# Splitting three of four second products of a macaron block's experts into reduced-precision parts, scans included

## The chip, the cores and the metric

The kernel runs on one core of one Trainium2 chip. The metric is device time in microseconds (us) of one launch; lower is better. TensorE is called PE below, VectorE DVE, ScalarE ACT, GpSimd POOL and SyncE (which here only issues DMAs) SP, as in the profile.

## The reference

Hidden states of 2 x 1024 tokens by 128 channels pass through half a mixture of experts, an attention layer with a recurrent state, and the same half mixture of experts again (same weights):

```python
x = x + 0.5 * ffn(layernorm(x))
x = x + attn(layernorm(x))
x = x + 0.5 * ffn(layernorm(x))

# ffn: 8 experts, all computed, two kept by a gate; F = 512
top_w, top_idx = top_k(softmax(x @ router_w.T), 2); top_w /= sum(top_w) + 1e-9
h = relu(einsum('tc,efc->tef', x, w1) + b1)        # first product
y = einsum('tef,ecf->tec', h, w2) + b2             # second product
out = sum over the two kept experts of top_w * y

# attn: token-shifted mixes -> r, w, k, v, g; 4 heads, 16 x 32 state each
o_t = r_t . (S + bonus * k_t v_t);  S = exp(-exp(w_t)) * S + k_t v_t   # scan over time
out = (groupnorm(o) * silu(g)) @ W_o.T
```

All is float32.

## The kernel before

**Layout.** Channels lie on partitions and tokens along the free axis, in blocks of 512 tokens. There are four such blocks of tokens; each goes through the experts twice, so there are `BLOCKS = 8` expert blocks. Expert block k has `SLOTS = 32` slots, one for each of 8 experts times `FC = 4` chunks of 128 hidden units. Slot n runs from 0 to 255 (`ALL = 256`), and `n % 4` is the chunk.

**A slot.** In slot n PE computes the first product of chunk n (`ffn_up(n)`, L229) and the second product of chunk n - `LAG` (`ffn_down`, L244, with `LAG = 2`). The first product is already made of three matmuls on split operands: each float32 factor is the sum of a high part rounded to the `F32R` type and the rest, and lo x hi, hi x lo and hi x hi are added in PSUM (L240 to L242). The second product is one plain float32 matmul (L251), which the hardware runs as two passes. ACT turns the PSUM bank `U[n % 2]` into `hid` (ReLU with bias, L443). `ffn_up(n)` waits until the ReLU of slot n - 2 is done, since there are two `U` banks.

**Experts' outputs.** After four chunks DVE multiplies `Y` by a gate row (`combine(g)`, L610, g = expert count) into `gy`, and POOL adds that to `xT` (L730). Both are called in slot `combine_slot(g)` = 4g + 6. The gate rows for a block are written to DRAM and read back broadcast over partitions into `G`, two blocks of eight experts deep, by SP (`gates_to_rows`, L180), whose queue is strictly in the written order.

**Attention.** Four attention units (`UNITS`) are laid over the slots: unit i starts in slot `UNIT[i]`, and step t of it is issued by each engine at the end of its slot `UNIT[i] + t`. The first 16 steps are the preamble (layernorm, mixes `mus`, projections). Steps 16 to 31 (`T_SC` on) are the scan: in each, PE spreads v (two `F32R` matmuls, L326 and L327), DVE multiplies by k (L629) and scans over 512 tokens (L637), and POOL multiplies the state by q into `qs` (L741). `v_spread(m)` waits for scan m - 3. In every fourth of these slots PE also reduces four `qs` tiles (L335), which waits for POOL's `qs` of two slots earlier; the last of the four reductions is in step 33, and the steps behind it (variance, normalising, output) wait for it. Units 0 and 1 scan from zero, units 2 and 3 carry the state on.

**Routing.** `PREP[k]` is the slot where the layernorm, the split of the input and the routing of expert block k begin; the routing's five steps on small tiles (`route`, L569 to L601) run on DVE in slots `PREP[k] + 8` to `+ 12`.

Every engine runs its own instructions in the order in which the loop over n writes them: on DVE `combine`, then `prepare` (routing among it), then `attend`; on ACT the ReLU of the slot first, then the rest. No planner reorders anything. The weights of experts 0 to 3 are loaded first, then the gate rows of block 0, then experts 4 to 7.

Of the kernel before, what the change touches and what calls it, by code (L numbers as in the profile page):

```python
# [11 lines left out]
P = 128  # L12
NB = 2
# [22 lines left out]
T_VAR, T_NORM, T_OUT = T_PO + 2, T_PO + 2, T_PO + 6  # L36
# [34 lines left out]
def combine_slot(g):  # L71

    return 4 * g + {0: 9}.get(g, 6)


def program(nc, xT_in, wexp_in, small_in, const_in, gate_dram, out):
    with ExitStack() as ctx:
# [31 lines left out]
        G = sb("G", [P, NB, E, NT])  # L109
# [35 lines left out]
        g_in = [[sem(f"g_in{b}{k}") for k in range(NQ)] for b in range(NB)]  # L145
# [6 lines left out]
        up, h_f, down = sem("up"), sem("h_f"), sem("down")  # L152
# [13 lines left out]
        def _(sp):  # L166
# [43 lines left out]
            gates_to_rows(1)  # L210
# [15 lines left out]
        def _(pe):  # L226
# [112 lines left out]
            def attend(i, t):  # L339
                if t == 0:  # L340
                    pe.wait_ge(acc, (i + 1) * E)
                    if i >= 1:
                        pe.wait_ge(x_att, i)
# [73 lines left out]
        def _(act):  # L417
# [21 lines left out]
            def relu(n):  # L439
# [3 lines left out]
                act.activation(hid[:, n % HS, :], U[n % 2][:, :], ACT.Relu, bias=w(W_B1 + n % (E * FC), 1)).then_inc(h_f, 1)  # L443
# [57 lines left out]
            for n in range(ALL):  # L501
# [12 lines left out]
        def _(dve):  # L514
# [87 lines left out]

            def combine(g):
                k, e = g // E, g % E
                dve.wait_ge(down, (g + 1) * FC)
                if e % EQ == 0:
                    dve.wait_ge(g_in[k % NB][e // EQ], 16 * (k // NB + 1))
                if g >= 2:
                    dve.wait_ge(acc, g - 1)
                dve.scalar_tensor_tensor(out=gy[:, g % 2, :], in0=Y[g % 2][:, :], scalar=w(W_B2 + e, 1),  # L610
                                         in1=G[:, k % NB, e, :], op0=ALU.add, op1=ALU.mult).then_inc(comb, 1)
# [28 lines left out]
            def attend(i, t):  # L640
# [61 lines left out]
            for n in range(ALL):  # L702
                if n in due:
# [20 lines left out]
        def _(pool):  # L724
            def add_y(g):
# [4 lines left out]
                pool.tensor_tensor(xT[:, h, b, :], xT[:, h, b, :], gy[:, g % 2, :], ALU.add).then_inc(acc, 1)  # L730

# [120 lines left out]
```

## Time and profile before

| | |
|---|---|
| median of three runs | 546.39 us (545.3 to 546.8) |
| the profiled execution | 545.84 us |
| its span, first to last instruction | 544.0 us |
| PE busy | 526.6 us, 97% |
| DVE busy | 318.1 us, 58% |
| ACT busy | 242.9 us, 45% |
| POOL busy | 188.1 us, 35% |

The profiled execution is 1.8 us longer than its span, and 0.55 us shorter than the median. Busy shares of DVE, ACT and POOL average over stretches with scans and stretches without; the trace has to be asked by stretch.

### The profile page before, as it was taken

To read this page: it belongs to the slowest core of one execution; us is meant where nothing else is said; L and a number is where in the kernel's file an instruction comes from. 1 tells how busy PE (TensorE), PEld (TensorE's weight loads), DVE (VectorE), ACT (ScalarE), POOL (GpSimd) and SP (SyncE) were. 2 spreads that over 40 slices of the span, in tenths; PEclk is the share of its full clock that TensorE was granted. 3 is DMA by queue.
4 is the path that set the end of the run, shared out by engine and by line. 5 is a ranking of instruction groups with operands and counts; after the bars stand their busy time and mean duration, and the time that the engine had idled before them with its cause. 6 is when DMAs were issued, how large, how long until landed. Compare 5 with 4: busy or idle time off the path is not lost.

```text
span 544.0 us, 5724 instructions
## 1 busy us (share of the span) xinstructions
PE 526.6 (97%) x1842; PEld 301.5 (55%) x1842; DVE 318.1 (58%) x629; ACT 242.9 (45%) x369; POOL 188.1 (35%) x220
## 2 busy tenths in 40 slices
PE   7999999999999999999999699999999999999996
PEld 4566664456556455555655355465465556666663
DVE  3554366498757638967775978474789843431111
ACT  2765454633256353325556223545542354544442
POOL 0031213367511426651151466211547612111221
PEclk9999999999999999999999989999999999999999
DMA  7264400400000400000040130000040000031000
GB/s 221 75 236 148 174 0 0 157 1 2 0 1 1 130 27 0 0 1 0 2 153 3 31 127 0 1 20 0 2 155 2 1 19 1 0 105 72 0 1 19
DMA packets 10350, 25.68 MB, mean 47 GB/s; under 512 B 2640, under 2 KB 2768, under 8 KB 10192
## 3 DMA queue, kind: packets, MB, share of 16 engines
q1 hardware_dynamic: 10320, 25.32, 13.7%
q8 instruction: 15, 0.25, 0.2%
q14 instruction: 15, 0.12, 0.1%
HBM read 24.13 MB, written 1.18 MB: 47 GB/s over the span
## 4 chain that ended last, share of the span: by engine, by line
PE 57%; issue 23%; POOL 14%; DVE 4%; ACT 1%; POOLq 0%; ACTq 0%; DVEq 0%
PE Y L251 25%; PE U L240 7%; PE U L242 7%; PE U L241 7%; POOL qs L741 6%; POOL xT L730 4%; POOL pool_a L754 2%; POOL pool_a L747 1%; PE A L266 1%; PE A L306 1%; PE A L260 1%; PE A L335 1%; POOL carry L738 1%; PE A L277 1%; PE Y L255 1%
## 5 line engine op out<-in xcount | busy, mean ns | idle before, releaser
L443 ACT ACTIVATE hid<-U,small 128x512 f32<-128x512 f32 x256 | 175.2, 686 | 251.0 <-PE U L242 249.8
L251 PE MATMUL Y<-hid,w 128*128 128x512 f32 x512 | 261.0, 591 | 0.1
L730 POOL TENSOR_TENSOR xT<-xT,gy 128x512 f32<-128x512 f32 x64 | 82.4, 1287 | 264.0 <-DVE gy L610 263.9
L240 PE MATMUL U<-xhi,w1lo 128*128 128x512 f32 x256 | 165.2, 645 | 1.5 <-ACT hid L443 0.9
L251 PEld LDWEIGHTS Y<-hid,w 128*128 128x128 f32 x512 | 96.4, 188 | 23.4 <-issue 1.4
L242 PE MATMUL U<-xhi,w1hi 128*128 128x512 f32 x256 | 101.2, 395 | 0.0
L241 PE MATMUL U<-xlo,w1hi 128*128 128x512 f32 x256 | 100.6, 393 | 0.0
L610 DVE SCALAR_TENSOR_TENSOR gy<-Y,small,G 128x512 f32<-128x512 f32 x64 | 47.4, 741 | 71.6 <-PE Y L251 71.4
L741 POOL TENSOR_TENSOR qs<-q,pool_a 128x512 f32<-128x512 f32 x64 | 75.9, 1186 | 34.3 <-DVE pool_a L637 34.3
L240 PEld LDWEIGHTS U<-xhi,w1lo 128*128 128x128 f32 x256 | 48.3, 189 | 65.4 <-issue 58.7
L241 PEld LDWEIGHTS U<-xlo,w1hi 128*128 128x128 f32 x256 | 48.6, 190 | 37.4 <-issue 35.0
L242 PEld LDWEIGHTS U<-xhi,w1hi 128*128 128x128 f32 x256 | 48.2, 188 | 11.2
L629 DVE TENSOR_TENSOR A<-A,kk 128x512 f32<-128x512 f32 x64 | 44.2, 691 | 14.0 <-PE A L327 13.9
L326 PE MATMUL A<-vlo,sel 128*128 128x512 f32 x64 | 50.3, 786 | 1.4 <-DVE pool_a L637 1.4
L637 DVE TENSOR_TENSOR_SCAN pool_a<-dec,carry,A 128x512 f32<-128x512 f32 x32 | 41.0, 1280 | 3.8 <-DVE A L629 0.5
L637 DVE TENSOR_TENSOR_SCAN pool_a<-dec,A 128x512 f32<-128x512 f32 x32 | 39.1, 1221 | 3.1
L754 POOL TENSOR_TENSOR pool_a<-pool_a,xa 128x512 f32<-128x512 f32 x20 | 21.2, 1090 | 26.9 <-DVE pool_a L654 26.9
L327 PE MATMUL A<-vhi,sel 128*128 128x512 f32 x64 | 25.2, 394 | 0.0
L335 PE MATMUL A<-qs,const 128*32 128x512 f32 x128 | 17.9, 631 | 6.3 <-POOL qs L741 6.0
L326 PEld LDWEIGHTS A<-vlo,sel 128*128 128x128 f32 x64 | 12.1, 188 | 17.9 <-issue 12.7
L682 DVE RECIPROCAL aw<-quk 128x512 f32<-128x512 f32 x4 | 13.4, 3353 | 12.7 <-ACT quk L493 12.7
L654 DVE SCALAR_TENSOR_TENSOR pool_a<-A,small,qs 128x512 f32<-128x512 f32 x20 | 13.9, 743 | 11.9 <-PE A L306 10.0
(116 smaller groups left out, 376.9 us busy)
## 6 DMA issues: line engine op xcount, KB each, us to landing
G<-gate_dram SPq DMA_DIRECT2D x32, 512.0 KB, 5.4
pool_a<-wexp_dram SPq DMA_DIRECT2D x8, 256.0 KB, 7.5
w<-wexp_dram SPq DMA_DIRECT2D x8, 256.0 KB, 7.5
xT<-xT_dram SPq DMA_DIRECT2D x4, 256.0 KB, 7.4
qs<-const_dram SPq DMA_DIRECT2D x1, 1024.0 KB, 10.4
out_dram<-xT SPq DMA_DIRECT2D x4, 256.0 KB, 2.5
small<-small_dram SPq DMA_DIRECT2D x1, 656.0 KB, 8.5
gate_dram<-gate_T SPq DMA_DIRECT2D x32, 4.0 KB, 1.4
```

The lines of the kernel that those rows point to most:

```text
L240: mm(dst, w1lo[:, e, f, :], xhi[:, k % NB, :], start=True, stop=False)
L241: mm(dst, w1hi[:, e, f, :], xlo[:, k % NB, :], start=False, stop=False)
L242: mm(dst, w1hi[:, e, f, :], xhi[:, k % NB, :], start=False, stop=True).then_inc(up, 1)
L251: mm(Y[g % 2][:, :], w2[:, g % E, f, :], hid[:, n % HS, :], start=(f == 0), stop=(f == FC - 1)).then_inc(down, 1)
L326: mm(dst, sel[:, j, :], vlo[:, :], start=True, stop=False)
L443: act.activation(hid[:, n % HS, :], U[n % 2][:, :], ACT.Relu, bias=w(W_B1 + n % (E * FC), 1)).then_inc(h_f, 1)
L610: dve.scalar_tensor_tensor(out=gy[:, g % 2, :], in0=Y[g % 2][:, :], scalar=w(W_B2 + e, 1), in1=G[:, k % NB, e, :], op0=ALU.add, op1=ALU.mu ...
L629: dve.tensor_tensor(bank, bank, kk[:, :], ALU.mult).then_inc(kv_r, 1)
L637: dve.tensor_tensor_scan(S[:, n % SS, 1:NT + 1], dec[:, :], bank, carry[:, b, m:m + 1] if h else 0.0, ALU.mult, ALU.add).then_inc(st_r, 1)
L730: pool.tensor_tensor(xT[:, h, b, :], xT[:, h, b, :], gy[:, g % 2, :], ALU.add).then_inc(acc, 1)
L741: pool.tensor_tensor(qs[:, n % QS, :], q[:, :], S[:, n % SS, 0:NT], ALU.mult).then_inc(qs_r, 1)
L754: pool.tensor_tensor(u[:, MIX[n], :], u[:, MIX[n], :], xa[:, b, 1:NT + 1], ALU.add).then_inc(u_r, 1)
```

## The change

From expert block 1 on, the second product of chunks 0, 1 and 2 of every expert (168 of 256) is computed like the first, from three matmuls on split operands. Chunk 3, and all of block 0, stay float32.

- **ACT** writes `hid` and, by a second ReLU of the same PSUM bank, `hid_hi` of type `F32R`.
- **DVE** computes `hid_lo = hid - hid_hi` (`split_h(n - 1)`, the first thing in its slot n).
- **PE** multiplies `w2lo` by `hid_hi`, `w2hi` by `hid_lo` and `w2hi` by `hid_hi`, and waits for `h_lo` instead of `h_f`.
- **w2's parts** for chunks 0 to 2 are made once during block 0 and stay in SBUF: ACT makes `w2hi`, POOL `w2lo`, one expert every four slots.
- **Gates** no longer have two blocks of eight rows but a ring of six: SP loads a pair of rows when the pair three before is used up. `gates_to_rows(1)` moves behind `rows_in(3)`.
- **Order:** `LAG` goes from 2 to 3, the combines one slot later, the starts in `PREP` and `UNIT` a few slots. The reciprocal of 512 columns is cut into four of 128, in four slots, and the steps behind it come later. In the units from 1 on, the wait for the previous unit's result moves from step 0 to step 7.

The function `in_parts` works out whether slot n belongs to a scan, but its result does not use it.

```diff
-PREP = [None, 6, 34, 74, 115, 125, 162, 206]
-UNIT = [36, 78, 119, 160]
-LAG = 2
+PREP = [None, 6, 34, 80, 114, 125, 167, 208]
+UNIT = [37, 79, 121, 163]
+LAG = 3
+FP, PS, GS = 3, 3, 6
-T_VAR, T_NORM, T_OUT = T_PO + 2, T_PO + 2, T_PO + 6
+T_VAR, T_NORM, T_OUT = T_PO + 2, T_PO + 3, T_PO + 10
 def combine_slot(g):
-    return 4 * g + {0: 9}.get(g, 6)
+    return 4 * g + {0: 10}.get(g, 7)
+def in_parts(n):
+    scans = any(start + T_SC - 3 <= n < start + T_PO for start in UNIT)
+    return n >= SLOTS and n % FC < FP
+def parts_to(n):
+    return sum(in_parts(k) for k in range(n))
+PARTS = [n for n in range(ALL) if in_parts(n)]
...
                 sp.wait_ge(g_out[k], 64)
-                if k >= NB:
-                    sp.wait_ge(comb, (k - 1) * E)
                 for k4 in range(NQ):
-                    sp.dma_start(G[:, b, k4 * EQ:(k4 + 1) * EQ, :].rearrange("p e n -> p (e n)"),
-                                 rows[b, k4].partition_broadcast(P)).then_inc(g_in[b][k4], 16)
+                    at = (k * E + k4 * EQ) % GS
+                    if k * E + (k4 + 1) * EQ > GS:
+                        sp.wait_ge(comb, k * E + (k4 + 1) * EQ - GS)
+                    sp.dma_start(G[:, at:at + EQ, :].rearrange("p e n -> p (e n)"),
+                                 rows[b, k4].partition_broadcast(P)).then_inc(g_in[at // EQ], 16)
...
-            gates_to_rows(1)
             rows_in(2)
...
             rows_in(3)
+            gates_to_rows(1)
...
-                pe.wait_ge(h_f, n + 1)
-                mm(Y[g % 2][:, :], w2[:, g % E, f, :], hid[:, n % HS, :], start=(f == 0), stop=(f == FC - 1)).then_inc(down, 1)
+                if in_parts(n):
+                    at = PARTS.index(n) % PS
+                    if g < 2 * E:
+                        pe.wait_ge(w2lo_s, g % E + 1)
+                    pe.wait_ge(h_lo, parts_to(n + 1))
+                    mm(dst, w2lo[:, g % E, f, :], hid_hi[:, at, :], start=first, stop=False)
+                    mm(dst, w2hi[:, g % E, f, :], hid_lo[:, at, :], start=False, stop=False)
+                    mm(dst, w2hi[:, g % E, f, :], hid_hi[:, at, :], start=False, stop=final).then_inc(down, 1)
+                else:
+                    pe.wait_ge(h_f, n + 1)
+                    mm(dst, w2[:, g % E, f, :], hid[:, n % HS, :], start=first, stop=final).then_inc(down, 1)
...
+                if in_parts(n):
+                    c = PARTS.index(n)
+                    if c >= PS:
+                        act.wait_ge(down, PARTS[c - PS] + 1)
+                    act.activation(hid[:, n % HS, :], U[n % 2][:, :], ACT.Relu, bias=bias)
+                    act.activation(hid_hi[:, c % PS, :], U[n % 2][:, :], ACT.Relu, bias=bias).then_inc(h_f, 1)
...
+            def split_w2(e):
+                act.wait_ge(w2_in[e], 16)
+                act.activation(w2hi[:, e].rearrange("p f n -> p (f n)"), w2[:, e, 0:FP].rearrange("p f n -> p (f n)"),
+                               ACT.Copy).then_inc(w2hi_s, 1)
...
+                if n % 4 == 2 and 1 <= n // 4 <= E:
+                    split_w2(n // 4 - 1)
...
+            def split_h(n):
+                if n < ALL and in_parts(n):
+                    c = PARTS.index(n) % PS
+                    dve.wait_ge(h_f, n + 1)
+                    dve.tensor_tensor(hid_lo[:, c, :], hid[:, n % HS, :], hid_hi[:, c, :], ALU.subtract).then_inc(h_lo, 1)
...
-                if t == T_NORM:
+                if T_NORM <= t < T_NORM + 4:
+                    c = (t - T_NORM) * P
                     dve.wait_ge(sd_r, i + 1)
+                    link(dve.reciprocal(aw[:, c:c + P], quk[:, c:c + P]))
+                if t == T_NORM + 3:
                     dve.wait_ge(ysc_r, i + 1)
-                    link(dve.reciprocal(aw[:, :], quk[:, :]))
...
             for n in range(ALL):
+                if n >= 1:
+                    split_h(n - 1)
                 if n in due:
                     combine(due[n])
```

## Rows read from the trace of the kernel before

**Rows 1.** The page: busy time of the engines, share of the span, instructions.

```profile
PE 526.6 (97%) x1842; PEld 301.5 (55%) x1842; DVE 318.1 (58%) x629; ACT 242.9 (45%) x369; POOL 188.1 (35%) x220
```

**Rows 2.** Timeline, PE, plain slots: start us, duration us, engine, line, instruction.

```profile
511.52 1.02 PE L251 MATMUL Y<-hid,w 128*128 128x512 f32 x2
...
512.61 0.39 PE L241 MATMUL U<-xlo,w1hi 128*128 128x512 f32 x1
512.83 0.39 PE L242 MATMUL U<-xhi,w1hi 128*128 128x512 f32 x1
513.07 1.02 PE L251 MATMUL Y<-hid,w 128*128 128x512 f32 x2
```

**Rows 3.** Busy time by stretch: length, PE, PEld, DVE, ACT, POOL, clock, DMA share, GB/s.

```profile
203.20:240.60 37.40, 36.93 (x139) 21.50 (x138) 32.63 (x36) 11.68 (x17) 24.91 (x37) 1.00 0.00 1
...
299.40:343.20 43.80, 37.94 (x139) 21.27 (x139) 36.43 (x45) 11.05 (x17) 25.74 (x34) 0.96 0.15 49
```

**Rows 4.** Timeline, DVE and one POOL row, inside the scans of units 0 and 2.

```profile
116.00 0.68 DVE L629 TENSOR_TENSOR A<-A,kk 128x512 f32<-128x512 f32 x1
...
119.76 0.67 DVE L629 TENSOR_TENSOR A<-A,kk 128x512 f32<-128x512 f32 x1
...
309.12 0.73 DVE L610 SCALAR_TENSOR_TENSOR gy<-Y,small,G 128x512 f32<-128x512 f32 x1
309.76 0.69 DVE L629 TENSOR_TENSOR A<-A,kk 128x512 f32<-128x512 f32 x1
310.56 1.28 DVE L637 TENSOR_TENSOR_SCAN pool_a<-dec,carry,A 128x512 f32<-128x512 f32 x1
311.75 0.67 DVE L629 TENSOR_TENSOR A<-A,kk 128x512 f32<-128x512 f32 x1
...
311.92 1.26 POOL L741 TENSOR_TENSOR qs<-q,pool_a 128x512 f32<-128x512 f32 x1 [0.20 <-DVE pool_a L637]
```

**Rows 5.** Timeline: first multiply and last reduction of units 0 and 3's scans.

```profile
109.62 0.70 DVE L629 TENSOR_TENSOR A<-A,kk 128x512 f32<-128x512 f32 x1 [2.10 <-PE A L327]
...
147.02 1.06 PE L335 MATMUL A<-qs,const 128*32 128x512 f32 x8 [0.48 <-POOL qs L741]
...
397.94 0.70 DVE L629 TENSOR_TENSOR A<-A,kk 128x512 f32<-128x512 f32 x1 [1.71 <-PE A L327]
...
435.71 1.06 PE L335 MATMUL A<-qs,const 128*32 128x512 f32 x8 [0.73 <-POOL qs L741]
```

**Rows 6.** Timeline, DVE and POOL, where both read two tiles of SBUF.

```profile
28.07 0.68 DVE L524 TENSOR_TENSOR w1lo<-pool_a,w1hi 128x512 fp32r<-128x512 f32 x1
28.23 3.07 POOL L730 TENSOR_TENSOR xT<-xT,gy 128x512 f32<-128x512 f32 x2 [26.98 <-DVE gy L610]
28.67 0.74 DVE L610 SCALAR_TENSOR_TENSOR gy<-Y,small,G 128x512 f32<-128x512 f32 x1
...
301.63 1.29 POOL L741 TENSOR_TENSOR qs<-q,pool_a 128x512 f32<-128x512 f32 x1 [3.38 <-DVE pool_a L637]
301.66 1.30 DVE L591 TENSOR_TENSOR rt<-const,rs 128x32 f32<-128x32 f32 x1
```

**Rows 7.** Timeline, ACT (and the PE row that releases one ReLU).

```profile
15.18 1.25 ACT L443 ACTIVATE hid<-U,small 128x512 f32<-128x512 f32 x2
...
81.19 1.28 ACT L436 ACT_TABLE_LOAD   x1
...
152.54 0.39 PE L242 MATMUL U<-xhi,w1hi 128*128 128x512 f32 x1
152.97 0.69 ACT L443 ACTIVATE hid<-U,small 128x512 f32<-128x512 f32 x1 [0.45 <-PE U L242]
```

**Rows 8.** Timeline and the page's DMA issues: the weights of expert 4.

```profile
24.63 0.78 SPq L176 DMA_DIRECT2D pool_a<-wexp_dram x1
...
32.65 0.62 ACT L420 ACTIVATE w1hi<-pool_a 128x512 fp32r<-128x512 f32 x1
...
pool_a<-wexp_dram SPq DMA_DIRECT2D x8, 256.0 KB, 7.5
```

More of the change, by code:

```diff
@@ L108, in program @@
         gate_T = sb("gate_T", [P, NB, 32])
-        G = sb("G", [P, NB, E, NT])
+        w2hi = sb("w2hi", [P, E, FP, P], F32R)
+        w2lo = sb("w2lo", [P, E, FP, P], F32R)
+        G = sb("G", [P, GS, NT])
+        hid_hi = sb("hid_hi", [P, PS, NT], F32R)
+        hid_lo = sb("hid_lo", [P, PS, NT], F32R)
         hid = sb("hid", [P, HS, NT])
@@ L144, in program @@
         g_out = [sem(f"g_out{k}") for k in range(BLOCKS)]
-        g_in = [[sem(f"g_in{b}{k}") for k in range(NQ)] for b in range(NB)]
+        g_in = [sem(f"g_in{k}") for k in range(GS // EQ)]
         w1hi_s, w1lo_s, sel_r, rw_r, setup, out_done = sem("w1hi_s"), sem("w1lo_s"), sem("sel_r"), sem("rw_r"), sem("setup"), sem("out_done")
@@ L249, in ffn_down @@
                     pe.wait_ge(comb, g - 1)
-                pe.wait_ge(h_f, n + 1)
-                mm(Y[g % 2][:, :], w2[:, g % E, f, :], hid[:, n % HS, :], start=(f == 0), stop=(f == FC - 1)).then_inc(down, 1)
+                dst, first, final = Y[g % 2][:, :], f == 0, f == FC - 1
+                if in_parts(n):
[9 more added lines that the diff above has]
+                    mm(dst, w2[:, g % E, f, :], hid[:, n % HS, :], start=first, stop=final).then_inc(down, 1)
             def keep_clock(n):
@@ L342, in attend @@
                     if i >= 1:
-                        pe.wait_ge(x_att, i)
+                        pe.wait_ge(ysc_r, i)
                     else:
@@ L351, in attend @@
                     pe.wait_ge(xm_r, i + 1)
+                    if i >= 1:
+                        pe.wait_ge(x_att, i)
                     mm(A[1][:, :], w(W_X1, P), xm, start=True, stop=True).then_inc(z_p, 1)
@@ L442, in relu @@
                     act.wait_ge(down, n - HS + 1)
-                act.activation(hid[:, n % HS, :], U[n % 2][:, :], ACT.Relu, bias=w(W_B1 + n % (E * FC), 1)).then_inc(h_f, 1)
+                bias = w(W_B1 + n % (E * FC), 1)
+                if in_parts(n):
[4 more added lines that the diff above has]
+                    act.activation(hid_hi[:, c % PS, :], U[n % 2][:, :], ACT.Relu, bias=bias).then_inc(h_f, 1)
+                else:
+                    act.activation(hid[:, n % HS, :], U[n % 2][:, :], ACT.Relu, bias=bias).then_inc(h_f, 1)
+            def split_w2(e):
+                act.wait_ge(w2_in[e], 16)
+                act.activation(w2hi[:, e].rearrange("p f n -> p (f n)"), w2[:, e, 0:FP].rearrange("p f n -> p (f n)"),
+                               ACT.Copy).then_inc(w2hi_s, 1)
             def prepare(k, t):
@@ L606, in combine @@
                 if e % EQ == 0:
-                    dve.wait_ge(g_in[k % NB][e // EQ], 16 * (k // NB + 1))
+                    dve.wait_ge(g_in[g % GS // EQ], 16 * (g // GS + 1))
                 if g >= 2:
@@ L610, in combine @@
                 dve.scalar_tensor_tensor(out=gy[:, g % 2, :], in0=Y[g % 2][:, :], scalar=w(W_B2 + e, 1),
-                                         in1=G[:, k % NB, e, :], op0=ALU.add, op1=ALU.mult).then_inc(comb, 1)
+                                         in1=G[:, g % GS, :], op0=ALU.add, op1=ALU.mult).then_inc(comb, 1)
             def prepare(k, t):
@@ L719, in _ @@
                     attend(i, n - UNIT[i])
+            split_h(ALL - 1)
             combine(BLOCKS * E - 1)
@@ L730, in add_y, with split_w2 @@
                 pool.tensor_tensor(xT[:, h, b, :], xT[:, h, b, :], gy[:, g % 2, :], ALU.add).then_inc(acc, 1)
+            def split_w2(e):
+                pool.wait_ge(w2hi_s, e + 1)
+                pool.tensor_tensor(w2lo[:, e].rearrange("p f n -> p (f n)"), w2[:, e, 0:FP].rearrange("p f n -> p (f n)"),
+                                   w2hi[:, e].rearrange("p f n -> p (f n)"), ALU.subtract).then_inc(w2lo_s, 1)
             def read_state(i, m):
@@ L777, in _ @@
                     add_y(due[n])
+                if n % 4 == 3 and 1 <= n // 4 <= E:
+                    split_w2(n // 4 - 1)
                 for i in range(UNITS):
```

3 lines of the change are left out of this document (2 added, 1 removed).

## The prediction

> **What bounds the kernel now.** I read the page's busy times first: PE is busy 97% of the span, DVE 58%, ACT 45%, POOL 35% [rows 1]. So PE sets the pace, and the change takes work from PE and gives it to ACT and DVE. The next view is PE's timeline in a plain slot, for what one conversion is worth. Then busy time by stretch, for who has room to take the work, because the shares of the page are averages: in the scan of unit 1 DVE is busy 32.63 of 37.40 us beside PE's 36.93 [rows 3]. There the room on DVE is 4.8 us, and in the scan of unit 2 DVE is already the one waited for: PE has 37.94 us of work in 43.80 [rows 3]. The last view is the timeline of DVE, POOL and ACT for the prices of what they are given, and of what holds them up.
>
> **The gain on PE.** From one second product to the next a plain slot takes 513.07 - 511.52 = 1.55 us [rows 2]. A split matmul follows the one before after 0.23 us (512.61, 512.83, 513.07) [rows 2]. The slot has three of them, 0.69 us, so the float32 product takes 0.86 us, and three split ones in its place 0.69: 0.17 us saved for each conversion, 168 x 0.17 = 28.6 us if PE stayed the bound in all slots. A plain slot becomes 1.38 us. The page "TensorE: Matmul & The Clock Gate" of the Trainium skill (back-to-back issue gap) gives 512 columns 216 ns at the full clock; the trace does not agree, since its split matmuls stand 0.23 us apart at a granted clock of 1.00. By that page's figure three would take 0.65 us and a conversion save 0.21.
>
> **The scans.** In each scan slot DVE does a multiply and a scan of 512 columns. Where DVE doesn't wait, these two take 1.88 us in units 0 and 1 (two pairs from 116.00 to 119.76) and 1.99 us in units 2 and 3 (309.76 to 311.75); a combine costs the queue 0.64 us (309.12 to 309.76) [rows 4]. The new subtraction has a twin in the old kernel, the subtraction for w1's low part: same shape and types, 0.68 us, and the next instruction starts 28.67 - 28.07 = 0.60 us after it [rows 6]. Four slots then cost DVE 4 x 1.88 + 0.64 + 3 x 0.60 = 10.0 us (10.4 in units 2 and 3). The four take PE about 37.4 / 4 = 9.3 us now, and 8.8 after three conversions. So DVE becomes the bound for the whole scan. PE may run up to three slots ahead, but that helps nothing: the last reduction needs the sixteenth scan, and steps behind it need the reduction.
>
> I take each unit from its first multiply to its last reduction. Behind the sixteenth scan, POOL's multiply comes once more behind a subtraction: 0.1 + 0.60 + 0.1 + 1.26 [rows 4, 6], 2.1 us.
> - Unit 0: 16 x 1.88 + 11 x 0.60 + 4 x 0.64 + 2.1 = 41.4 us, where it was 147.02 - 109.62 = 37.4 [rows 5]: +4.0.
> - Unit 1, with one combine less inside: 40.7 against 37.4 [rows 3]: +3.3.
> - Unit 2: 16 x 1.99 + 6.6 + 2.6 + 2.1 = 43.1 against 43.8 [rows 3]: -0.7. There the old kernel had the routing of block 5 between its first scans; the new starts leave one routing step in the first scan slot, about +1. Together +0.3.
> - Unit 3: 16 x 1.99 + 6.6 + 1.9 + 2.1 = 42.4, and one routing step of about 0.9, against 435.71 - 397.94 = 37.8 [rows 5]: +5.5.
>
> Sum +13.1 us. Each of these stretches holds 17 second products, 51 conversions in all, whose gain is thereby spent. Bounds: if each hand-over around a subtraction cost 0.1 us more, +4.4; if POOL won none of its waits at the end, -2.4. So +10.7 to +17.5.
>
> **Outside the scans.** 168 - 51 = 117 conversions at 0.17: -19.9 us. DVE has 12 subtractions of 0.60 more in some 16 slots there, which are not its bound.
>
> **ACT.** A ReLU starts 152.97 - 152.54 = 0.43 us after the third split matmul of its slot, 0.89 us after the slot's start, and two of them take 1.25 us [rows 7]. They end at 2.14; the next use of that bank is two slots on, at 2.76 instead of 3.10. With 0.15 us for the signal the margin is 0.45 us, where it was 3.10 - 0.89 - 0.69 - 0.15 = 1.37 with one ReLU. An ACT table load is 1.28 us [rows 7], 1.5 with the small activation behind it. It was hidden under 1.37 us of margin and ACT's gaps; in the middle of three double ReLUs it now costs 1.5 - 0.23 (gap) - 0.45 = 0.8 us. Twelve such loads lie from block 1 on. Slot 41 (with the copy of `xa` beside it) and slots 121 and 122 (two in a row) cost about 1.4 and 1.5; those in the variance steps have a float32 product of 0.86 us of PE in the same slot and cost 0.3 each, those beside a chunk 3 next to nothing. Sum +4.0, bounds 0 and 12 x 0.8 = 10.
>
> **POOL and DVE at one port.** A small DVE op on two SBUF tiles that started 0.03 us behind a POOL multiply took 1.30 us and ended with it [rows 6]. The other way round, two POOL adds beside the subtraction at 28.07 took 3.07 instead of 2 x 1.28 us [rows 6]. The subtraction that is added reads two SBUF tiles, so it belongs to this kind. In the scans it stands right behind a scan in DVE's queue: the next DVE instruction starts at 311.75, and POOL, which must be told first, at 311.92 [rows 4]. DVE comes first, POOL loses 0.60 us, and POOL's load of 1.45 to 2.1 us fits in DVE's 2.5. That is why the sum above has no wait for it. In the preamble POOL's five adds meet the subtractions, and PE waits for those adds: 0.5 us a unit, +2.0, bounds 0 and 5. The Trainium skill's page "SBUF — State Buffer" (who interferes with whom) says the same as these rows, that issue order decides which of the two blocks for the whole instruction; it is the ground of the second rival.
>
> **What else moves.** The one-slot-later combines and `LAG = 3` move products in PE's queue and add none; the rings `hid` (five) and `hid_hi` (three) are free a slot or more before they are wanted. The reciprocal in four pieces takes a 3.35 us block off DVE's queue but is waited for only later. The gate ring: SP now stands in block 0 before the fourth pair until the second combine is done. That combine started at 28.67 [rows 6] and comes about a slot later; SP then issues a pair and the weights of expert 4 at about 30.3 instead of 24.63, with one pair in front of them instead of four [rows 8]. ACT took them at 32.65 [rows 8]. At a landing of 4.5 us (the median behind four pairs is 7.5 [rows 8]) they are there at 35; ACT's margin in block 0 (one ReLU a slot, and the routing of block 1 on PE) hides all but 0.3. Bounds 0 and 4. Later pairs are asked for 20 slots before use, over 27 us. ACT's and POOL's splits of w2 (eight each, in block 0) lie in idle time.
>
> **Sum.** -19.9 + 13.1 + 4.0 + 2.0 + 0.3 = -0.5 us on the span: 543.5. Plus 1.8 outside it: 545.3 for a profiled execution, and with 0.55 to the median 545.9 us. That is no change. Gain and loss are both real and of one size.
>
> **Rivals.**
> - *Margins hold better than priced* (faster). The table loads and the port cost nothing, POOL's last wait neither: -19.9 + 10.7 + 0.3 = -8.9, a time of 537.5. For it: ACT is idle in over half of each stretch now. Against it: the margin of 0.45 us is under a third of a table load. By the skill's 0.21 us for a conversion it would be 4.7 us lower still. Chance 0.25, with times from 534 to 542.
> - *POOL wins the port in the scans* (slower). If a ready signal reaches POOL before DVE begins its subtraction, that waits 1.1 to 1.3 us for the multiply. It decides as soon as DVE's start behind a scan falls later than POOL's, 0.17 us on. Four times in ten of 44 subtractions: 18 x 1.2 = +21, 567 us; always: +53. Against it stands the order of starts. Chance 0.10.
> - *ACT's ring takes PE's place* (slower). Each table load costs 0.8, the preambles give PE no cover, and the hand-overs cost DVE 0.1 each: -0.5 + 6 + 3 + 4.4 = +13, 559 us. Decides if the pair of ReLUs ends later than 2.4 us after the slot's start. Chance 0.15, times from 551 to 560.
> - *It doesn't do what it says.* The flag for scans is worked out and not used, so scans are included, as the change is described; I find nothing idle in it.
>
> **How the numbers follow.** Forecast 545.9, chance 0.50, times from 542 to 551. About 0.3% (1.6 us) is what a measurement of this kernel tells from no change: 544.75 to 548.0 counts as the same. Of the forecast's 0.50, 0.13 falls below, 0.22 inside and 0.15 above. Faster 0.13 + 0.25 = 0.38, same 0.22, slower 0.15 + 0.10 + 0.15 = 0.40. The range leaves out the port rival and the fast rival's lower end: 536 to 560.
>
> **What would show it.** In plain slots of the last block: 1.38 us a slot, 1.55 for chunk 3. In each scan stretch: DVE busy over 95% and PE waiting, 41 to 43 us from first multiply to last reduction. The subtraction at 0.68 us there; 1.2 or more would be the port rival, and a POOL multiply 0.6 us longer the forecast's order. PE waiting for ReLUs around slots 41, 115 to 125 and 215, by 4 us in all. The prediction is wrong if the scans stay at 37 us, or if plain slots show PE idle.

## The result and the profile after

The changed kernel takes 557.53 us (556.78 to 558.3, four runs) beside 545.93 us for the kernel before on the same chip: ratio 1.0211, 95% interval 1.0189 to 1.0234. It is slower by 11.6 us, about 2%, where no change was forecast. The time lies inside the range given; the direction was missed.

The page's busy times, in the order of [rows 1], and the granted clock in 40 slices:

```profile
PE 512.1 (92%) x2010; PEld 335.0 (60%) x2010; DVE 425.1 (76%) x809; ACT 341.4 (61%) x545; POOL 219.9 (40%) x228
...
PEclk9999999999999899999999989899997999999998
```

PE has 14.5 us less of busy time than before and is busy 92% of a longer span. DVE has 107 us more, ACT 98 us more. The stretches of [rows 3] answer with these (length, PE, PEld, DVE, ACT, POOL, clock, DMA share, GB/s), first the scan of unit 0, then the stretch up to the next scan, the scan of unit 3 and the rest:

```profile
110.02:152.16 42.14, 35.24 (x152) 23.74 (x150) 39.52 (x49) 19.36 (x31) 31.15 (x36) 1.00 0.07 26
152.16:210.26 58.10, 55.89 (x213) 34.53 (x214) 46.17 (x97) 39.57 (x64) 14.51 (x12) 0.97 0.05 14
...
413.64:457.44 43.80, 35.64 (x141) 23.06 (x140) 39.94 (x49) 17.82 (x28) 28.87 (x34) 0.92 0.07 25
457.44:556.50 99.06, 94.08 (x377) 68.81 (x377) 57.27 (x108) 70.69 (x111) 21.89 (x17) 0.97 0.12 41
```

In the scans DVE is busy 91 to 96% (over 95 was forecast) and PE waits 6.9 of 42.1 us in unit 0's. What was not forecast is in the second row: DVE is busy 46.2 of 58.1 us there, and the stretch is longer than before (203.22 - 147.02 = 56.2 us), although the products in it are cheaper.

Plain slots near the end show what a conversion gives PE (timeline, PE, one slot from L277 to L277):

```profile
521.26 0.40 PE L277 MATMUL Y<-hid_hi,w2lo 128*128 128x512 f32 x1
521.50 0.39 PE L278 MATMUL Y<-hid_lo,w2hi 128*128 128x512 f32 x1
521.73 0.40 PE L279 MATMUL Y<-hid_hi,w2hi 128*128 128x512 f32 x1
521.96 0.40 PE L261 MATMUL U<-xhi,w1lo 128*128 128x512 f32 x1
...
522.66 0.40 PE L277 MATMUL Y<-hid_hi,w2lo 128*128 128x512 f32 x1
```

A single slot takes 1.40 us, against the 1.55 of [rows 2]. Single starts are too coarse for a difference this small, so I take slots 228 to 252 as well, by the start of the third matmul of their first products (L242 before, L263 after). They take 37.12 us before (494.27 to 531.39) and 34.28 after (509.61 to 543.89), with 18 conversions among them: 0.16 us for a conversion (0.158), where 0.17 was forecast. The split matmuls stand 0.23 us apart.

A scan step with a subtraction, timeline of DVE and POOL (the counterpart of [rows 4]):

```profile
133.37 1.22 DVE L691 TENSOR_TENSOR_SCAN pool_a<-dec,A 128x512 f32<-128x512 f32 x1
134.51 0.67 DVE L655 TENSOR_TENSOR hid_lo<-hid,hid_hi 128x512 fp32r<-128x512 f32 x1
134.65 0.56 POOL L802 COPY carry<-pool_a 128x1 f32<-128x1 f32 x1 [0.70 <-DVE pool_a L691]
135.09 0.74 DVE L664 SCALAR_TENSOR_TENSOR gy<-Y,small,G 128x512 f32<-128x512 f32 x1
135.17 1.09 POOL L805 TENSOR_TENSOR qs<-q,pool_a 128x512 f32<-128x512 f32 x1
135.75 0.69 DVE L683 TENSOR_TENSOR A<-A,kk 128x512 f32<-128x512 f32 x1
...
137.83 0.18 POOL L802 COPY carry<-pool_a 128x1 f32<-128x1 f32 x1 [0.31 <-DVE pool_a L691]
```

DVE's instructions follow each other without a gap. The subtraction starts 0.14 us ahead of POOL and takes its normal 0.67 us; it is POOL's copy of one element per partition that is held, 0.56 us instead of the 0.18 of the last row, where no subtraction stands behind the scan. Units 2 and 3 have no such copy at that place, and there POOL's multiply itself is held, 1.45 us for a subtraction where it takes 1.09 to 1.10 without one:

```profile
417.61 0.67 DVE L655 TENSOR_TENSOR hid_lo<-hid,hid_hi 128x512 fp32r<-128x512 f32 x1
417.77 1.45 POOL L805 TENSOR_TENSOR qs<-q,pool_a 128x512 f32<-128x512 f32 x1 [0.55 <-DVE pool_a L691]
```

So a subtraction costs POOL 0.36 to 0.38 us. One subtraction of some fifty in the scans is held instead (1.75 us, at 354.69).

The program of slots is the same in all experiments on the changed kernel, so its span can be cut at the same marks: head (to the first multiply of unit 0's scan), each scan (start of the first multiply to start of the last reduction), the gaps between scans, and the tail. All are us of the one profiled execution, which can lie 1 to 2 us off the kernel's median, read from the timelines of L683 (multiply) and L366 (reduction) or their lines in that kernel:

| kernel | head | scan 0 | gap | scan 1 | gap | scan 2 | gap | scan 3 | tail | scans | outside |
|---|---|---|---|---|---|---|---|---|---|---|---|
| before | 109.6 | 37.4 | 56.2 | 37.4 | 58.8 | 43.7 | 54.8 | 37.8 | 108.3 | 156.3 | 387.7 |
| after | 110.0 | 42.1 | 58.1 | 41.3 | 61.5 | 42.9 | 57.7 | 43.8 | 99.1 | 170.2 | 386.3 |
| e1 no conversion | 111.0 | 37.4 | 56.2 | 37.4 | 58.0 | 37.5 | 57.5 | 36.8 | 104.5 | 149.1 | 387.2 |
| e2 not in scans | 109.7 | 37.4 | 58.4 | 37.4 | 60.4 | 37.4 | 55.3 | 36.8 | 97.8 | 149.0 | 381.6 |
| e3 only in scans | 111.3 | 42.1 | 57.2 | 41.3 | 60.4 | 43.1 | 58.2 | 42.1 | 104.2 | 168.5 | 391.2 |
| e4 no subtraction | 109.2 | 36.1 | 53.7 | 35.7 | 56.7 | 36.7 | 55.0 | 35.7 | 97.1 | 144.2 | 371.6 |
| e6 POOL subtracts | 110.4 | 37.4 | 55.6 | 37.4 | 58.7 | 37.4 | 55.1 | 36.8 | 98.4 | 149.0 | 378.3 |
| e7 filler on PE | 110.0 | 42.1 | 58.1 | 41.3 | 62.4 | 42.7 | 56.3 | 42.1 | 97.5 | 168.2 | 384.3 |
| e13 not in preambles | 110.3 | 37.4 | 56.1 | 37.4 | 58.2 | 37.5 | 55.2 | 36.8 | 97.8 | 149.1 | 377.5 |

The schedule before has other start slots, so its single gaps do not compare one by one; its sums do.

### The profile page after: what moved, and what is told of

The parts are those of the page before. It is cut to its first block, busy times and chain, and to the rows that moved or that the text cites. A ratio compares the mean times of both kernels' runs of the same rounds, so it can differ in the third digit from the quotient of the medians.

```text
span 556.5 us, 6459 instructions
## 1 busy us (share of the span) xinstructions
PE 512.1 (92%) x2010; PEld 335.0 (60%) x2010; DVE 425.1 (76%) x809; ACT 341.4 (61%) x545; POOL 219.9 (40%) x228
## 4 chain that ended last, share of the span: by engine, by line
PE 44%; issue 23%; DVE 14%; POOL 14%; ACT 4%; POOLq 0%; DVEq 0%; ACTq 0%
PE Y L282 8%; POOL qs L805 7%; PE U L261 6%; PE U L263 6%; PE U L262 6%; POOL xT L789 4%; PE Y L277 3%; PE Y L278 3%; PE Y L279 3%; DVE hid_lo L655 3%; POOL carry L802 2%; DVE pool_a L708 2%; DVE gy L664 1%; DVE xnt L590 1%; DVE aw L736 1%
## 5 line engine op out<-in xcount | busy, mean ns | idle before, releaser
L655 DVE TENSOR_TENSOR hid_lo<-hid,hid_hi 128x512 fp32r<-128x512 f32 x168 | 121.2, 727 | 34.2 <-ACT hid_hi L482 33.5
L261 PE MATMUL U<-xhi,w1lo 128*128 128x512 f32 x256 | 139.5, 545 | 3.0 <-ACT hid L484 1.5
L482 ACT ACTIVATE hid_hi<-U,small 128x512 fp32r<-128x512 f32 x168 | 114.7, 683 | 0.0
L484 ACT ACTIVATE hid<-U,small 128x512 f32<-128x512 f32 x88 | 60.4, 688 | 68.1 <-PE U L263 67.7
L263 PE MATMUL U<-xhi,w1hi 128*128 128x512 f32 x256 | 102.0, 398 | 0.0
L805 POOL TENSOR_TENSOR qs<-q,pool_a 128x512 f32<-128x512 f32 x64 | 85.0, 1329 | 31.7 <-DVE pool_a L691 31.7
L282 PE MATMUL Y<-hid,w 128*128 128x512 f32 x176 | 89.8, 591 | 0.0
L261 PEld LDWEIGHTS U<-xhi,w1lo 128*128 128x128 f32 x256 | 48.8, 191 | 57.9 <-issue 38.5
L277 PE MATMUL Y<-hid_hi,w2lo 128*128 128x512 f32 x168 | 68.0, 405 | 1.9 <-DVE hid_lo L655 1.9
L278 PE MATMUL Y<-hid_lo,w2hi 128*128 128x512 f32 x168 | 66.8, 397 | 0.0
L279 PE MATMUL Y<-hid_hi,w2hi 128*128 128x512 f32 x168 | 66.3, 394 | 0.0
L263 PEld LDWEIGHTS U<-xhi,w1hi 128*128 128x128 f32 x256 | 48.9, 191 | 11.5
L683 DVE TENSOR_TENSOR A<-A,kk 128x512 f32<-128x512 f32 x64 | 44.0, 687 | 2.4 <-PE A L358 2.2
L366 PE MATMUL A<-qs,const 128*32 128x512 f32 x128 | 19.9, 698 | 26.7 <-POOL qs L805 26.6
L691 DVE TENSOR_TENSOR_SCAN pool_a<-dec,A 128x512 f32<-128x512 f32 x32 | 39.1, 1221 | 3.1
L277 PEld LDWEIGHTS Y<-hid_hi,w2lo 128*128 128x128 f32 x168 | 32.2, 192 | 11.8 <-DVE hid_lo L655 2.9
## 6 DMA issues: line engine op xcount, KB each, us to landing
G<-gate_dram SPq DMA_DIRECT2D x32, 512.0 KB, 3.8
```

Source lines behind the costliest of these rows:

```text
L261: mm(dst, w1lo[:, e, f, :], xhi[:, k % NB, :], start=True, stop=False)
L263: mm(dst, w1hi[:, e, f, :], xhi[:, k % NB, :], start=False, stop=True).then_inc(up, 1)
L277: mm(dst, w2lo[:, g % E, f, :], hid_hi[:, at, :], start=first, stop=False)
L278: mm(dst, w2hi[:, g % E, f, :], hid_lo[:, at, :], start=False, stop=False)
L279: mm(dst, w2hi[:, g % E, f, :], hid_hi[:, at, :], start=False, stop=final).then_inc(down, 1)
L282: mm(dst, w2[:, g % E, f, :], hid[:, n % HS, :], start=first, stop=final).then_inc(down, 1)
```

## Experiments: the parts of the change

My theory after the result: the scans cost what was forecast, and the loss is outside them, in DVE's queue, where the forecast had priced the subtractions at nothing. The rivals: the moved schedule itself, ACT's second ReLU, the half clock, or a spill of the scans' backlog.

**e1, the schedule alone.**

```diff
-    return n >= SLOTS and n % FC < FP
+    return False
```

> The changed kernel with no chunk converted: the new starts, LAG of 3, combines one slot later, the reciprocal in four pieces, the gate ring of six and the (here unused) parts of w2 stay. Theory A (the moves are free, all loss comes from the conversions): within 1.5 us of the kernel before, 545 to 548. Theory B (the later starts and later steps themselves lengthen the chains between attention units): 552 or more.

Measured 538.5 us, ratio to the kernel before 0.9859 (0.9845 to 0.9874). Neither theory had it: the moves are worth 7.7 us. Busy time by stretch of this kernel, the gap behind scan 0 and then the scan of unit 2:

```profile
148.44:204.69 56.25, 56.25 (x194) 30.71 (x195) 34.87 (x78) 29.53 (x46) 14.73 (x13) 1.00 0.08 23
...
299.90:337.50 37.60, 37.15 (x140) 21.66 (x138) 33.43 (x37) 11.68 (x17) 25.66 (x34) 1.00 0.09 29
```

The scan of unit 2 takes 37.5 us where it took 43.7 (table; [rows 3] cut it at 43.8), and PE hardly waits in it. The routing of block 5 stands ahead of that scan now (its last instruction starts at 299.90 us, the scan's first multiply at 300.06) and no longer between its steps. That is 6.2 of the 7.7 us; unit 3's scan gives 1.0, and the rest lies outside the scans. So the changed kernel does not lose 11.6 us by its conversions but 19.0, and 7.7 us of other gain hide part of it.

**e2 and e3, the conversions of one kind of slot.**

```diff
-    return n >= SLOTS and n % FC < FP
+    return n >= SLOTS and n % FC < FP and not scans   # e2
+    return n >= SLOTS and n % FC < FP and scans       # e3
```

> The conversions are left out in the slots of the scans (the unused flag is used). In the changed kernel's trace the four stretches from first multiply to last reduction are 14 us longer in sum than before, and what lies outside them is 1.4 us shorter where 14 were forecast. Theory A (what is lost outside the scans is made there, by DVE's and ACT's queues in the preambles): only the 14 us come back, 543 to 545. Theory B (the outside loss is the scans' doing, by DVE's backlog at their ends and by the half clock that PE's waits bring): the outside loss goes too, 531 to 536.

> Conversions only in the slots of the scans. Each stretch again 41 to 44 us. Theory A (costs add up): before plus 14, 558 to 562. Theory B (the scans' conversions also cost outside): 564 or more. If the sum of this kernel's and the other's distance from the kernel with no conversion is that of the changed kernel, the two parts are independent.

Measured 532.1 us (0.9742, 0.9723 to 0.9761) and 563.4 us (1.0316, 1.0289 to 1.0343). e2 falls into the range of its theory B and e3 between its two ranges, but both expectations started from the kernel before, without the 7.7 us of the schedule, so neither range decides anything; what does is the comparison with e1. Against e1, conversions outside the scans give 6.4 us and those in the scans cost 24.9; the sum, 538.5 - 6.4 + 24.9 = 557.0, is the changed kernel's 557.5. The two parts add up. The profiled executions of e3 and e1 differ by 23.5 us, and the table splits that: the scans go from 149.1 to 168.5 us, +19.4, and 4.0 us fall outside them (391.2 against 387.2). The changed kernel against e2 shows the same spill, 386.3 - 381.6 = 4.7 us.

**e10 and e11, one or two chunks in the scans.**

```diff
+    return n >= SLOTS and n % FC < (1 if scans else FP)   # e10
+    return n >= SLOTS and n % FC < (2 if scans else FP)   # e11
```

> Conversions outside the scans as before, and chunk 0 alone in the slots of the scans. Theory A (DVE has 9.1 us for four slots, needs 8.2 to 8.6 and with one subtraction 8.8 to 9.2: PE stays the bound): each scan stretch 36.5 to 37.5 us, the whole 529 to 532. Theory B (each subtraction in a scan costs its 0.6 us whatever the room, since multiply and scan depend on each other): stretches 38.5 to 40 us, the whole 536 to 541.

> Chunks 0 and 1 in the slots of the scans. Theory A (four slots cost DVE 9.4 us in units 0 and 1, 9.8 in units 2 and 3, more than PE's 8.9): stretches of about 39, 38.5, 41 and 40.5 us, the whole 540 to 545. Theory B (only the third subtraction is too much): 529 to 533.

Measured 532.8 us (0.976, 0.9745 to 0.9774) and 542.0 us (0.9926, 0.9907 to 0.9946). The scan stretches are 37.6, 37.1, 37.9 and 37.5 us with one chunk, and 39.7, 39.1, 40.3 and 39.9 with two, beside forecasts of 39, 38.5, 41 and 40.5. With three, 42.1, 41.3, 42.9 and 43.8. e10 is within 1 us of e2, which has none in the scans: one conversion in four slots costs and gives about nothing; each further one is added to the time by DVE. The room is about one subtraction, as the forecast's arithmetic has it: 8.2 to 8.6 us of DVE's work in four slots, beside the 9.1 that they take PE.

## Experiments: who makes the loss outside the scans

**e4, no subtraction.** DVE's instruction runs for the first three converted chunks only, so this kernel leaves out the low part of the rest; PE then waits for ACT.

```diff
-                    pe.wait_ge(h_lo, parts_to(n + 1))
+                    pe.wait_ge(h_lo, min(PS, parts_to(n + 1)))
+                    pe.wait_ge(h_f, n + 1)
...
+                    if c != PARTS.index(n):
+                        return
                     dve.wait_ge(h_f, n + 1)
...
```

> All conversions stay on PE and ACT, but DVE's subtraction is left out after the first three (the low part of the hidden units keeps those values). Theory A (DVE's queue makes nearly all loss, in and outside the scans): scans back to 35 to 37 us each, and the gain of 28.6 us less about 4 for ACT: 520 to 526. Theory B (ACT's second ReLU makes the loss outside): 532 to 538.

Measured 517.8 us (0.9482, 0.9467 to 0.9496), below both ranges. All conversions at 0.158 us are 26.5 us, from 538.5 to 512.0. Of the 5.8 us that are missing about half lies in the scans (144.2 us against e1's 149.1, where 51 conversions would give 8.1); the rest is ACT's second ReLU and what is not told apart. The subtraction costs 557.5 - 517.8 = 39.7 us (40.7 in the profiled executions, 14.7 of it outside the scans, 386.3 against 371.6, and 9.2 in the first two gaps). 21 us of the first gap in the changed kernel, and 21 us that begin equally far behind scan 0 in this one (columns as above):

```profile
162.00:183.00 21.00, 19.51 (x86) 13.84 (x85) 20.41 (x48) 16.45 (x27) 4.26 (x3) 1.00 0.09 26
```

```profile
155.00:176.00 21.00, 20.78 (x94) 15.02 (x93) 16.43 (x43) 16.63 (x27) 4.26 (x3) 1.00 0.08 26
```

DVE is busy 20.41 of 21.00 us in the changed kernel, with layernorm statistics and normalising for two layernorms, the reciprocals, mixes, combines and subtractions. The mean of 80% over the gap hides that. The timeline shows what PE waits for (DVE, and the PE rows below):

```profile
178.95 0.68 DVE L702 TENSOR_TENSOR qs<-xa 128x512 f32<-128x512 f32 x1
179.66 1.68 DVE L703 SCALAR_TENSOR_TENSOR qs<-qs,small,xa 128x512 f32<-128x512 f32 x1
181.26 0.68 DVE L655 TENSOR_TENSOR hid_lo<-hid,hid_hi 128x512 fp32r<-128x512 f32 x1
181.86 0.68 DVE L596 TENSOR_TENSOR xlo<-A,xhi 128x512 fp32r<-128x512 f32 x1
...
182.69 0.25 PE L308 MATMUL A<-rwh,xlo 128*128 128x16 f32 x1 [1.26 <-DVE xlo L596]
...
187.22 0.63 PE L263 MATMUL U<-xhi,w1hi 128*128 128x512 f32 x1
```

`xlo` for block 3's router comes behind a mix and a subtraction; PE waits 1.26 us, does 16-column matmuls for 0.9 us, and from 184.89 to 188.31 its granted clock is 0.50 (0.63 us a matmul instead of 0.39). That slot, 86, takes 7.04 us from its third matmul (L263) to the next slot's, and 7.51 in e2; in e1 and e4 it takes 4.48 and 4.47. The mix is held to 1.67 us in e1 as well, by one of POOL's adds, so that is not the difference; there `xlo` follows it at once:

```profile
175.22 1.67 DVE L703 SCALAR_TENSOR_TENSOR qs<-qs,small,xa 128x512 f32<-128x512 f32 x1
176.81 0.68 DVE L596 TENSOR_TENSOR xlo<-A,xhi 128x512 fp32r<-128x512 f32 x1
```

**e5, one ReLU.** The second activation runs for the first three converted chunks only; for the rest this kernel leaves it out, and `hid_hi` keeps those values.

```diff
-                    act.activation(hid_hi[:, c % PS, :], U[n % 2][:, :], ACT.Relu, bias=bias).then_inc(h_f, 1)
...
+                    if c < PS:
+                        first = act.activation(hid_hi[:, c % PS, :], U[n % 2][:, :], ACT.Relu, bias=bias)
+                    first.then_inc(h_f, 1)
```

> The changed kernel with ACT's second ReLU left out after the first three (the high part of the hidden units keeps those values); DVE's subtraction and PE's products stay. Theory A (DVE's queue makes the loss, ACT about 4 us that hide behind DVE's): 552 to 557. Theory B (ACT's double ReLU also holds up DVE's subtractions, and so costs more than its own 4 us): 545 to 550.

Measured 554.4 us (1.0145, 1.0122 to 1.0168), 3.2 us below the changed kernel: theory A. Where ACT costs PE time can be read slot by slot, from the third matmul of a slot's first product to the next slot's. Four slots that stand just behind an ACT table load are longer in the changed kernel than in e5: slot 43 takes 2.12 us against 1.39, slots 75 and 159 take 1.87 against 1.38, slot 217 takes 1.64 against 1.39, 2.0 us in sum. In the view of the waits of the changed kernel (engine, line, releaser: us in total, times, longest) PE's waits for the second ReLU are

```profile
PE U L261 <- ACT hid_hi L482: 0.9, 3, 0.5
```

The rest of the 3.2 us is not told apart; e5's PE also has some 7 us less at the lower clock (mean clock 0.985 against 0.979). So ACT, with 98 us more work, is worth 2 to 3 us; DVE, with 107 us more, 39.7.

**e8, the subtraction last in DVE's slot.**

```diff
-                if n >= 1:
-                    split_h(n - 1)
                 if n in due:
                     combine(due[n])
...
                     attend(i, n - UNIT[i])
+                if n >= 1:
+                    split_h(n - 1)
```

> The changed kernel with DVE's subtraction at the end of its slot's work instead of its beginning, so that it stands behind the layernorm, mix and projection steps on which PE waits next. Theory A (in the preambles it is DVE's total load that counts): within 2 us of the changed kernel, 555 to 559. Theory B (it is the place: each step on PE's path stands behind a subtraction of 0.6 us, and behind the ReLU that the subtraction waits for): 3 to 8 us less, 549 to 554.

Measured 572.1 us (1.0468, 1.0445 to 1.049). Both theories fall: 14.6 us slower than the changed kernel. The view of the waits for this kernel, and below it for the changed one:

```profile
PE Y L277 <- DVE hid_lo L655: 38.8, 46, 2.8
```

```profile
PE A L366 <- POOL qs L805: 26.6, 15, 2.9
PE A L308 <- DVE xlo L596: 2.2, 2, 1.3
PE Y L277 <- DVE hid_lo L655: 1.9, 3, 1.1
```

A subtraction at the end of a slot comes too late for the product of its chunk, two slots on, 46 times. Of the two places the slot's beginning is by far the better; places between them were not tested.

**e9, the preparation of block 3 in slot 74,** on e2, to part it from unit 1's preamble.

```diff
-PREP = [None, 6, 34, 80, 114, 125, 167, 208]
+PREP = [None, 6, 34, 74, 114, 125, 167, 208]
```

> Conversions outside the scans only, and the preparation of expert block 3 starts in slot 74, as before the change, instead of slot 80, one slot behind the start of attention unit 1. Theory A (the stretch between the scans of units 0 and 1 loses because two layernorms, a routing and the preamble meet in DVE's queue): that stretch goes from 58.4 us to 54 to 56, the whole from 532.1 to 528 to 530. Theory B (DVE's load is as large wherever the preparation lies): 531 to 534.

Measured 533.2 us (0.9762, 0.9746 to 0.9779), and the gap became 59.1 us, not shorter: theory A falls. My guess is that the work met other work of DVE, the end of unit 0; that is not shown.

**e13 and e14, no or one conversion in the two crowded preambles,** on e2:

```diff
+    crowded = 73 <= n < 92 or 113 <= n < 134
-    return n >= SLOTS and n % FC < FP and not scans
+    return n >= SLOTS and n % FC < FP and not scans and not crowded         # e13
+    return n >= SLOTS and n % FC < (1 if crowded else FP) and not scans     # e14
```

> Conversions neither in the scans nor in slots 73 to 91 and 113 to 133, where a layernorm and routing of an expert block and the preamble of unit 1 or 2 share DVE's queue. Some 30 conversions fewer, worth 5 us of PE at 0.17. Theory A (those conversions cost more than they give): the stretches between the scans fall from 58.4 and 60.4 us to the 56.2 and 58.0 of the kernel without conversions, the whole from 532.1 to 526 to 529. Theory B (the loss of these stretches is not tied to the conversions in them but comes from the ones ahead of them): 533 to 537.

> As the last one, but chunk 0 is still converted in those slots. Theory A (it is DVE's load there that decides, and one subtraction in four slots still fits): the two stretches 0.8 us shorter each than without, the whole 525 to 528. Theory B (any subtraction there stands ahead of a step on PE's path): 528 to 532.

Measured 528.2 us (0.967, 0.9655 to 0.9684) and 527.7 us (0.9657, 0.9641 to 0.9673). With 30 conversions fewer the kernel is 3.9 us faster than e2, and the two gaps are 56.1 and 58.2 us. So these 30 cost 4.1 us outside the scans in the trace and use up their gain of 4.7 us (30 x 0.158) as well: 8.8 us. e13 leaves out all three parts of a conversion, so it does not say which part costs; e4 does. It has these conversions, with ACT's second ReLU but without the subtraction, and its two gaps are 4.7 and 3.7 us shorter than e2's (53.7 and 56.7 against 58.4 and 60.4), 8.4 in sum. e14's gaps are 55.7 and 58.2 us; the 0.5 us by which it is faster than e13 are within their spread, so whether one subtraction fits stays open. e14 beats both kernels: 3.4% faster than before, 29.8 us faster than the change.

## Experiments: port and clock

**e6, POOL subtracts,** on e2: `split_h` moves from DVE's slot to the beginning of POOL's.

```diff
-                    dve.wait_ge(h_f, n + 1)
-                    dve.tensor_tensor(hid_lo[:, c, :], hid[:, n % HS, :], hid_hi[:, c, :], ALU.subtract).then_inc(h_lo, 1)
+                    pool.wait_ge(h_f, n + 1)
+                    pool.tensor_tensor(hid_lo[:, c, :], hid[:, n % HS, :], hid_hi[:, c, :], ALU.subtract).then_inc(h_lo, 1)
```

> Conversions outside the scans only, and POOL does the subtraction in DVE's place, in the same slots. Theory A (the two preambles of units 1 and 2 lose because DVE's queue is full there): the stretches between the scans go from 58.4 and 60.4 us to 54 to 57, the whole from 532.1 to 522 to 527. Theory B (POOL's subtraction, 1.3 us at the port that both share, holds up DVE's ops on two SBUF tiles and POOL's own five adds): 530 to 538.

Measured 530.0 us (0.9705, 0.9691 to 0.972). It is 2.1 us faster than e2, at the fast edge of theory B. The two gaps are 4.5 us shorter in sum (55.6 and 58.7 us against 58.4 and 60.4), head and tail 1.3 longer, and its execution is 2.8 us longer than its span where the others' are 1.8. DVE is relieved, but e4's gaps are 3.9 us shorter still.

**e12, three changes together,** on e6: chunk 0 in the scans with DVE's subtraction and a semaphore of its own, and block 3 prepared in slot 74.

```diff
-PREP = [None, 6, 34, 80, 114, 125, 167, 208]
+PREP = [None, 6, 34, 74, 114, 125, 167, 208]
...
-    return n >= SLOTS and n % FC < FP and not scans
+    return n >= SLOTS and n % FC < (1 if in_scans(n) else FP)
...
-                    pe.wait_ge(h_lo, parts_to(n + 1))
+                    pe.wait_ge(h_sc if in_scans(n) else h_lo, parts_to(n + 1, in_scans(n)))
```

> Conversions outside the scans with the subtraction on POOL, chunk 0 in the scans with the subtraction on DVE, and the preparation of block 3 in slot 74. If the three gains add up (2 us for POOL, 1 to 3 for chunk 0, 2 to 4 for the start): 522 to 528, the fastest of all kernels that compute the whole. If POOL's subtractions meet its other work in the earlier preparation: 528 to 532.

Measured 538.1 us (0.9849, 0.9826 to 0.9873), above both ranges. The gains do not add up; the gap behind scan 0 alone takes 63.8 us, where e6 has 55.6. Its timeline (POOL, DVE and PE):

```profile
179.23 3.75 POOL L803 TENSOR_TENSOR hid_lo<-hid,hid_hi 128x512 fp32r<-128x512 f32 x3
...
179.57 0.99 DVE L634 TENSOR_TENSOR rt<-const,rs 128x32 f32<-128x32 f32 x1
180.60 1.19 DVE L636 SCALAR_TENSOR_TENSOR rt<-rt 128x32 f32<-128x32 f32 x1
...
182.04 0.97 DVE L639 TENSOR_TENSOR rt<-rt,rs 128x32 f32<-128x32 f32 x1
...
184.86 2.04 PE L389 MATMUL A<-qs,small 128*128 128x512 f32 x2 [3.67 <-issue]
```

POOL does three subtractions in a row, and three small steps of the routing (such steps take 0.19 us alone) wait for one each, to 1.0 to 1.2 us. DVE's mix comes late and PE stands 3.67 us. The granted clock falls to 0.50 during that stand (183.47 us), and over the whole gap it is 0.92, where e6 has 1.00; how the 8.2 us divide between port and clock is not shown. The row names no releaser; the code there waits for that mix. This is [rows 6] repeated: whoever starts first holds the port. By the Trainium skill ("SBUF — State Buffer", who interferes with whom) the loser blocks for the whole instruction; the trace agrees, since L634 ends at 180.56, just behind POOL's first subtraction (180.52). I had put work on an idle engine that shares a port with the full one.

**e7, filler ahead of PE's waits.**

```diff
+                if slot >= SLOTS:
+                    pe.wait_ge(h_f, slot)
+                    for _ in range(4):
+                        mm(U[(slot + 1) % 2][:, :], w1hi[:, 0, 0, :], xhi[:, 0, :], start=True, stop=True)
                 pe.wait_ge(qs_r, i * VG + 4 * n + 4)
```

> The changed kernel with four more matmuls of 512 columns (0.93 us, into a bank that the next slot overwrites) ahead of PE's wait in each of the 16 reductions; nothing else waits for them. PE waits 1.2 to 2.9 us there now. Theory A (PE's waits in the scans bring the half clock, which then costs up to 1.7 us a stretch; there are five such stretches and one of double length): fewer stretches at half clock, 552 to 556. Theory B (the clock's stretches cost nothing because DVE sets the pace while they last): same number of us as the changed kernel, 556 to 559, whatever the clock does.

Measured 552.8 us (1.0115, 1.0096 to 1.0133), 4.7 us below the changed kernel, with 64 matmuls more. The mean granted clocks of the changed kernel and of this one:

```profile
core 0: 556.5 us, clock 0.979
```

```profile
core 0: 552.5 us, clock 0.994
```

A mean of 0.979 at levels of 1 and 0.5 is 2 x 0.021 x 556.5 = 23 us at 1.2 GHz; here it is 7, and 5 in the kernel before. By stretch, 17 of the 23 us lie in the scans of units 2 and 3 or up to 4 us behind them (324.84 to 328.25, 355.56 to 358.97, 423.83 to 430.65, 457.96 to 461.37), 3.4 in slot 86, and 3.0 at the end, where PE is done. Here those 17 us are gone: the clock is 1.00 through both scans; slot 86 keeps its 3.4, and 3.4 new ones lie in the gap behind scan 1. So PE's waits in these two scans bring the lower clock, though the waits in the scans of units 0 and 1 (1.25 to 2.6 us each) left the clock at 1.00. Theory A holds. The scan of unit 3, at a clock of 0.92 in the changed kernel, goes from 43.8 to 42.1 us, the gap ahead of it from 57.7 to 56.3 and the tail from 99.1 to 97.5.

## Why the prediction was wrong

**Right.** PE as the bound before, and the turn to DVE in the scans: 42.1, 41.3, 42.9 and 43.8 us, forecast 41.4, 40.7, 44.1 and 43.3, in sum +13.9 against +13.1. Its arithmetic also gave e11's stretches within 0.7 us. Unit 3's agreement is in part luck: without the lower clock, in e3 and e7, that scan takes 42.1 us. The port in the scans: DVE comes first, the subtraction takes 0.67 us there, POOL pays, though 0.36 to 0.38 us and not 0.60. The weights of expert 4: ACT waits for them (2.8 us in the view of the waits), but the head is 110.0 us against 109.6 with one slot more in it.

**The step that failed** is one sentence: "DVE has 12 subtractions of 0.60 more in some 16 slots there, which are not its bound." The forecast gives no row for it, and had itself warned of the page's means. The runs show DVE busy 20.41 of 21.00 us in the first of the two crowded preambles, PE waiting for `xlo` behind a subtraction, and 8.8 us lost in the two together (e2 against e13; e4 shows that the subtraction is the part that costs). It is the largest part of the 12.2 us that are missing outside the scans (387.7 - 13.6 forecast, 386.3 measured).

**Left out altogether** was what the scans do beyond their ends: 4.0 to 4.7 us outside them (e3 against e1, the changed kernel against e2). The lower clock after PE's waits has a share in it; e7 gives back 2.0 of it outside and 2.0 inside the scans. I had priced the clock nowhere in the forecast. How the rest of the spill divides between DVE's backlog and the clock is not shown.

**Mis-sized** was the gain of a conversion, 0.158 for 0.17 us, 1.4 us over 117: the forecast read two steps of about 0.23 us, each given to 0.01 us, and multiplied their error by three and by 117. Mis-sized too was ACT, 4.0 us forecast. The mechanism was right, for the slots that are longer stand behind table loads, but 2.0 us in four slots are what the trace shows, not 4.0 in twelve. Slot 43, behind the load with the copy of `xa` beside it, pays 0.73 us and not 1.4. The 0.15 us for the signal has no row: before the change PE's `U` matmul starts 0.05 us after the ReLU that it waits for (at 15.90 and 256.3 us).

Together, outside the scans: from e1 to e2 come 104 conversions, -16.4 us, the preambles, +8.8, and +2.0 for ACT, POOL and what is not told apart, in sum the measured -5.6. From e2 to the changed kernel comes the spill, +4.7, which already has in it the gain of some 13 conversions that the flag for scans counts to the scans but whose products lie outside the stretches. That gives the -0.9 us by which the changed kernel differs from e1 there.

**Of the rivals,** the time fell into the range of "ACT's ring takes PE's place", but not by that mechanism, which e5 excludes: without the second ReLU the kernel is still at 554.4. The rival on the port occurred once in the scans, in unit 2's; e12 shows what it looks like where POOL does come first. Outside the scans nine subtractions take 1.1 to 1.6 us instead of 0.68, eight of them beside POOL's adds in the preambles; what they cost is not shown.

**A gain went unnoticed:** the moved starts. The forecast compared the new scan of unit 2 with the old 43.8 us [rows 3] and saw 0.7 us. It did not say that without conversions the same move would give 6.2. Against the right baseline, e1, the scans are 21.1 us longer and not 13.9. So a schedule worth 7.7 us and conversions outside the scans worth 6.4 were shipped together with ones that cost 24.9.

## What to carry to other kernels

When work moves from a full engine to a half-idle one, cut the receiver's busy time into pieces as short as the slack of the waits behind it, here one preamble, and add the new work piece by piece; a mean of 80% was 97% over the 21 us that mattered. Convert only where the receiver has room: e14 converts three chunks of four in 100 of the 224 slots, one of four in 40 and none in 84, and is 5.3% faster than the kernel that converts three in all of them. And test a change that also moves the schedule with its main part switched off, since the two can have opposite signs.

## What the runs showed of the hardware

- In the scans of units 2 and 3, seven waits of PE of 0.5 to 2.9 us went with 17 us at the lower clock; four more matmuls ahead of each wait, 0.93 us of useless work, left none there and made the kernel 4.7 us faster. Eight waits of 1.25 to 2.6 us in the scans of units 0 and 1 left the clock at 1.00.
- A DVE subtraction of 512 columns on two SBUF tiles holds even a POOL copy of one element per partition: 0.56 instead of 0.18 us.
- A reciprocal of 128 columns takes 0.95 us, so four cost 3.8 where one of 512 took 3.35; that is 0.45 us a unit for letting other work in between.
